# A gate's last 32 inner columns: small tiles against four copies in two f32r terms

## The reference, cut to what matters

```python
h = jnp.tanh(xx @ A).reshape(5, B * T, 32)
miu = jnp.einsum('smk,skc->smc', h, Bp).reshape(5, B, T, C) + lam
x5 = x[None] + b_a[None] * miu
...
g = jnp.tanh(g_in @ Wg1) @ Wg2
y = wkv6(r, k, v, w, u)
...
return yn * g @ Wo.T
```

## Time and profile before

| | us |
|---|---|
| median of 3 runs | 668.16 |
| the three runs | 666.41, 668.16, 670.31 |
| the profiled execution, its own time | 671.27 |
| its span, first to last instruction | 670.0 |
| TensorE matmul busy | 575.6 (86%) |
| TensorE weight load busy | 490.5 (73%) |
| VectorE busy | 433.1 (65%) |
| ScalarE busy | 280.8 (42%) |
| GpSimd busy | 221.2 (33%) |
| mean granted clock of TensorE | 0.929 of full speed |

### The profile page before, as it was taken

How to read it: one execution, slowest core, us unless ns; L and a number is a source line. 1 busy time by engine, 2 the same in 40 slices (tenths; PEclk the granted TensorE clock), 3 DMA queues, 4 the chain that set the end, 5 groups by cost and what they waited for, 6 DMA issues and landing times.

```text
span 670.0 us, 19207 instructions
## 1 busy us (share of the span) xinstructions
PE 575.6 (86%) x7602; PEld 490.5 (73%) x7602; DVE 433.1 (65%) x1091; ACT 280.8 (42%) x596; POOL 221.2 (33%) x178
## 2 busy tenths in 40 slices
PE   2799471649689999999999989999989999989795
PEld 1688351528478979898989878989878989777674
DVE  5784571626576767676767686767686767686432
ACT  3576020021235454545454525454535454535331
POOL 3120037150413333333333323433333333332413
PEclk9889575677699999999999999999999999999989
DMA  8988893280212323333333323333223333121422
GB/s 275 248 257 225 238 302 122 74 233 15 54 25 65 64 65 60 70 57 72 58 71 57 72 41 65 65 65 64 65 42 65 65 66 65 26 41 26 64 32 32
DMA packets 61962, 61.42 MB, mean 92 GB/s; under 512 B 6321, under 2 KB 56242, under 8 KB 61730
## 3 DMA queue, kind: packets, MB, share of 16 engines
q1 hardware_dynamic: 48002, 45.31, 25.5%
q0 software_dynamic: 12896, 14.50, 14.7%
q10 hardware_dynamic: 976, 0.38, 0.2%
HBM read 41.36 MB, written 23.14 MB: 96 GB/s over the span
## 4 chain that ended last, share of the span: by engine, by line
PE 70%; DVE 10%; issue 6%; SPq 5%; DMA 3%; another core or an unknown queue 3%; POOL 2%; ACT 1%; DVEq 0%; ACTq 0%; POOLq 0%
PE F L563 11%; PE F L555 10%; PE G L376 7%; PE LL L444 6%; PE YB L532 4%; PE YB L488 4%; PE G L345 4%; PE G L392 3%; PE YB L486 3%; PE G L407 2%; SPq L1539 2%; PE YB L513 2%; PE YB L517 2%; DVE mix L865 2%
## 5 line engine op out<-in xcount | busy, mean ns | idle before, releaser
L1417 POOL DMA_INDIRECT out<-ys,dst_row x39 | 65.7, 1685 | 208.9 <-DVE ys L981 196.0
L901 DVE COPY_PREDICATED AP_<-msk,LL 128x256 f32<-128x256 uint32 x96 | 51.2, 533 | 59.4 <-PE LL L444 37.2
L865 DVE SCALAR_TENSOR_TENSOR mix<-G,vec,ba 128x256 f32<-128x256 f32 x160 | 69.6, 477 | 25.8 <-PE G L345 15.4
L555 PEld LDWEIGHTS F<-xsT,w1s 128*128 128x128 f32 x624 | 73.8, 192 | 7.4 <-issue 5.4
L563 PE MATMUL F<-w,hsT 128*128 x312 | 78.1, 394 | 0.8 <-ACT hsT L1268 0.8
L555 PE MATMUL F<-xsT,w1s 128*128 128x128 f32 x624 | 78.2, 278 | 0.7 <-ACT xsT L1250 0.7
L1268 ACT ACTIVATE hsT<-F,b1c 128x128 f32<-128x128 f32 x156 | 44.7, 368 | 67.8 <-PE F L555 67.7
L444 PEld LDWEIGHTS LL<-R,K 64*64 64x64 f32 x2560 | 47.9, 139 | 31.1 <-issue 20.0
L444 PE MATMUL LL<-R,K 64*64 64x32 f32 x2560 | 56.6, 226 | 15.9 <-DVE D L919 12.3
L563 PEld LDWEIGHTS F<-w,hsT 128*128 128x128 f32 x312 | 58.2, 193 | 10.1 <-issue 1.4
L917 DVE TENSOR_TENSOR R<-R,D 128x256 f32<-128x256 f32 x112 | 48.4, 432 | 25.0 <-issue 19.9
(11 more groups left out here) (149 smaller groups left out, 1098.4 us busy)
## 6 DMA issues: line engine op xcount, KB each, us to landing
cd<-cd_d SPq DMA_DIRECT2D x32, 320.0 KB
w<-in_W SPq DMA_DIRECT2D x16, 512.0 KB, 8.9
cd_d<-cd SPq DMA_DIRECT2D x32, 160.0 KB, 3.3
b2t<-in_b SPq DMA_DIRECT2D x39, 128.0 KB
w<-in_x SPq DMA_DIRECT2D x8, 512.0 KB, 9.8
xn_d<-w SPq DMA_DIRECT2D x8, 512.0 KB
out<-in_x SPq DMA_DIRECT2D x8, 512.0 KB
out<-res POOLq DMA_DIRECT2D x16, 256.0 KB, 4.5
```

The source lines that it names most:

```text
L555: i1 = pe.matmul(FB[:, k * P:(k + 1) * P], w1s[:, cc, k, :], xsT[:, cc, :], start=(cc == 0), stop=(cc == 1))
L865: i1 = dve.scalar_tensor_tensor(mixed_in(u, c, n, cc), bk[:, cc * UN:(cc + 1) * UN], cvec(LAM + CC * n, cc), ba[:, cc, :, :].rearrange("p ...
L901: dve.copy_predicated(to, m, now.rearrange("p g (n t) -> p g n t", t=B)).then_inc(s["a"])
L1417: pool.indirect_dma_start(io["out"], bass.IndirectOffsetOnAxis(dst_row[:, f:f + 1], 0), ys[:, f % 2, :], None, compute_op=ALU.add).then_in ...
```

## The change

The last 32 inner columns are laid out four times on the host: `Wg1` becomes 256x256 (its last 32 columns four times) and `Wg2` 256x256 (its last 32 rows four times). `gate_down` is then four f32 products of 128x256, the second two of which give four copies of the rest's 32 rows on 128 partitions, for all tokens. The tanh covers 512 columns. ScalarE copies the rest's half of it, rounded to f32r, into `tgh`, which lies where `con` held its triangle and ones. VectorE's `gate_terms` makes `tgx` from it: in copies 1 and 3 the difference to the rounded value, in copies 0 and 2 the value itself, rounded (the factor is a new column LOW of `con`, 0 or -1). `Wg2`'s copies are brought to two terms as well: raw rows go to the still unused `sq`, VectorE casts them to f32r into `wg2x` and puts the difference to the rounded value in rows 64 to 127, once, in `centred`. The product of `tgx` and `wg2x` over 128 rows is then the sum of the four term pairs, as two f32r products of 128x256 in `gate_up`, in place of eight small f32 ones. `gate_up` waits for `gate_terms` (semaphore tx) where it waited for the tanh, and the copy waits for the terms of the unit before (tx) since `tgh` is single. SP issues three loads fewer.

```diff
-        wg1 = sb("wg1", [P, CC, GR])
-        wg2 = sb("wg2", [P, 2, C])
+        wg1 = sb("wg1", [P, CC, 2 * P])
+        wg2x = sb("wg2x", [P, C], F32R)
+        wg2 = sb("wg2", [P, C])
...
-        tg = sb("tg", [P, 2, UN + UB * QT])
+        tg = sb("tg", [P, 2, 2 * UN])
+        tgx = sb("tgx", [P, 2, UN], F32R)
...
+        tgh = con[:, TRI:TRI + UN]
...
             def gate_down(u, c):
...
-                for cc in range(CC):
-                    pe.matmul(bk[:, 0:UN], wg1[:, cc, 0:P], mixed_in(u, c, 4, cc), start=(cc == 0), stop=(cc == 1))
-
-                for cc in range(CC):
-                    for g in range(4):
-                        i1 = pe.matmul(bk[LORA * g:LORA * (g + 1), UN:UN + UB * QT], wg1[:, cc, P:GR], mixture(u, c, 4)[:, cc, :, QT * g:QT * (g + 1)],
-                                       start=(cc == 0), stop=(cc == 1), tile_position=(0, LORA * g))
+                for k in range(2):
+                    for cc in range(CC):
+                        i1 = pe.matmul(bk[:, k * UN:(k + 1) * UN], wg1[:, cc, k * P:(k + 1) * P], mixed_in(u, c, 4, cc), start=(cc == 0), stop=(cc == 1))
...
             def gate_up(u, c):
                 q = seq(u, c)
-                pe.wait_ge(s["tg"], q + 1)
+                pe.wait_ge(s["tx"], q + 1)
+                if not q:
+                    pe.wait_ge(s["gx"], 2)
...
-                    for g in range(4):
-                        at = slice(QT * g, QT * (g + 1))
-                        i1 = pe.matmul(BB[at, b * C:(b + 1) * C], tg[at, u, UN + QT * b:UN + QT * (b + 1)], wg2[at, 1, :],
-                                       start=False, stop=(b == UB - 1), tile_position=(QT * g, QT * g))
+                    i1 = pe.matmul(BB[:, b * C:(b + 1) * C], tgx[:, u, b * P:(b + 1) * P], wg2x[:, :], start=False, stop=(b == UB - 1))
...
             def centred():
...
+                raw = sq[:, 0, :]
+                dve.tensor_copy(wg2x[:, :], raw).then_inc(s["gx"])
+                dve.wait_ge(s["gx"], 1)
+                at = slice(2 * LORA, 4 * LORA)
+                dve.tensor_tensor(wg2x[at, :], raw[at, :], wg2x[at, :].bitcast(F32), ALU.subtract).then_inc(s["gx"])
...
+            def gate_terms(u, c):
+
+                dve.wait_ge(s["th"], seq(u, c) + 1)
+                rest = tg[:, u, UN:2 * UN]
+                dve.scalar_tensor_tensor(tgx[:, u, :], tgh, con[:, LOW:LOW + 1], rest, ALU.mult, ALU.add).then_inc(s["tx"])
...
                 mixed(u, c + 1, 0)
                 added(u, c + 1, 0)
+                gate_terms(*v)
                 mixed(u, c + 1, 1)
...
                 if q > 1:
                     act.wait_ge(s["gg"], q - 1)
-                act.activation(tg[:, u, :], bank(u, c, "tg")[:, 0:UN + UB * QT], ACT.Tanh).then_inc(s["tg"])
+                act.activation(tg[:, u, :], bank(u, c, "tg")[:, :], ACT.Tanh).then_inc(s["tg"])
+                act.wait_ge(s["tg"], q + 1)
+                if q:
+                    act.wait_ge(s["tx"], q)
+                act.activation(tgh.bitcast(F32R), tg[:, u, UN:2 * UN], ACT.Copy).then_inc(s["th"])
...
-                    (wg2[:, 0, :], io["Wg2"][0:P, :]), *((wg2[LORA * g:LORA * (g + 1), 1, :], io["Wg2"][P:GR, :]) for g in range(4)),
+                    (wg2[:, :], io["Wg2"][0:P, :]), (sq[:, 0, :], io["Wg2"][P:2 * P, :]),
...
+    four = lambda w, axis: np.concatenate([w] + 3 * [np.take(w, range(P, GR), axis)], axis)
...
-        "Wg1": g["a_Wg1"], "Wg2": g["a_Wg2"], "Wr": g["f_Wr"], "br": g["f_br"].reshape(E),
+        "Wg1": four(g["a_Wg1"], 1), "Wg2": four(g["a_Wg2"], 0), "Wr": g["f_Wr"], "br": g["f_br"].reshape(E),
```

More of the change, by code:

```diff
@@ L34 @@
 UN = UB * P
-QT = P // 4
 NU = 2 * NCH
@@ L48 @@
 SPARE = 3 * P
-NCONST = SPARE + 1
+LOW = SPARE + 1
+NCONST = LOW + 1
 RANK8 = 0
@@ L179, in program @@
             "cr0 cr1 "
-            "ba mm m x tA tw tB d km k vm v rm r gm tg "
+            "ba mm m x tA tw tB d km k vm v rm r gm tg th tx gx "
             "ru lev a gr big spread "
@@ L512, in gate_up @@
                 for b in range(UB):
-                    pe.matmul(BB[:, b * C:(b + 1) * C], tg[:, u, b * P:(b + 1) * P], wg2[:, 0, :], start=(b == 0), stop=False)
+                    pe.matmul(BB[:, b * C:(b + 1) * C], tg[:, u, b * P:(b + 1) * P], wg2[:, :], start=(b == 0), stop=False)
                 for b in range(UB):
-                    for g in range(4):
-                        at = slice(QT * g, QT * (g + 1))
-                        i1 = pe.matmul(BB[at, b * C:(b + 1) * C], tg[at, u, UN + QT * b:UN + QT * (b + 1)], wg2[at, 1, :],
-                                       start=False, stop=(b == UB - 1), tile_position=(QT * g, QT * g))
+                    i1 = pe.matmul(BB[:, b * C:(b + 1) * C], tgx[:, u, b * P:(b + 1) * P], wg2x[:, :], start=False, stop=(b == UB - 1))
                 i1.then_inc(s["gg"])
@@ L622, in tensor_program @@
                     ln_logits(j - 1)
-            pe.wait_ge(s["w"], 256)
+            pe.wait_ge(s["w"], 208)
             mixed(0, 0, 0)
@@ L744, in centred @@
                 wv3 = wv[:, :, :].rearrange("p c (h i) -> p (c h) i", i=HEAD)
-                dve.wait_ge(s["w"], 256)
+                dve.wait_ge(s["w"], 208)
                 dve.tensor_reduce(mwv, wv3, AX.X, ALU.add).then_inc(s["step"])
@@ L1068, in vector_program @@
             levels(0, 0, 2)
+            gate_terms(0, 0)
             mixed(1, 0, 1)
@@ L1086, in vector_program @@
             c = NCH - 1
+            gate_terms(1, c)
             levels(1, c, 0, 1)
@@ L1329, in scalar_program @@
             exponentials()
-            act.wait_ge(s["w"], 256)
+            act.wait_ge(s["w"], 208)
             decay_down(0, 0)
@@ L1602, in constants @@
     con[:, SPARE] = 1 + TOK + a
+    con[:, LOW] = -(a // LORA % 2)
     msk = np.zeros((P, len(LEVELS), LEAF), np.uint32)
```

## The result

The changed kernel takes **659.73 us** (median of 4 runs, 657.43 to 665.0), the kernel before 668.32 (4 runs, three of them the ones on record above): ratio 0.9873, 95% interval 0.9824 to 0.9922. The forecast of 666.3 (662.8 to 670.6) was too high: right in sign, wrong in size. Two more jobs in which the kernel before takes 668 and 670 gave 0.9839 [0.9798, 0.9880] and 0.9846 [0.9807, 0.9885]. In two other jobs the kernel before takes 638.0, and the ratio is 0.9923 [0.9903, 0.9943] and 0.9930 [0.9905, 0.9954]. The expectations speak of two chips, which isn't shown: the later slower jobs ran on chips numbered 7, 1 and 1, the faster ones on 1 and 14, and the first job's has no number.

The account below looks back on a forecast made before the run. TensorE was taken to bound 13 of the 14 halves, with waits elsewhere. Halves -3.1, half 0 +0.7, start +0.3 and +0.2, end 0 gave -1.9 us: 668.16 to 666.3, range 662.8 to 670.6.

Parts of the forecast that it names:

- gate_down +0.50, gate_up -0.85: TensorE in each half: gate_down from 1.32 to 1.82 us, gate_up from 2.05 to 1.20, net -0.35 where TensorE is the bound.
- the factor of four: The skill's up to 4x for dimensions of 32 or less; by it the change would cost TensorE +0.12 us a unit.
- The small tiles also cost something around them: TensorE time of 0.05 to 0.1 us a unit that start-to-start times give to the small tiles' neighbours.
- the first rival: No waits for z and mix 1, small tiles cost extra, start hides its part: -5.4 us, 662.8; chance 0.25.
- z, +0.07 a half: TensorE's gated_back would wait about 0.07 us for VectorE's z in each half, as gate_up gets 0.85 shorter.
- ScalarE, nothing: Longer tanh and added copy, +0.62 us on ScalarE, cost nothing in three-tile halves: out still ends 0.16 ahead of key_back.
- Mix 1 in two-tile halves, +0.14: gate_terms delays VectorE's mixed 1 by 0.4 us in two-tile halves, making it 0.14 late for TensorE's product.
- Halves -0.28 and -0.14, together -3.1: Change per half in us: nine three-tile halves at -0.28, four two-tile ones at -0.14, all but half 0.
- All of it arrives: The first rival's title: waits do not appear and small tiles cost extra; -5.4 us, 662.8; chance 0.25.
- Half 0, +0.7: Half 0: shorter gate_up earns nothing behind a wait; longer gate_down, partly at the low clock, costs +0.7 us.
- Start, +0.3, +0.16, and "I take nothing" for the loaded stretches: Start: Wg2 operations less saved loads +0.3 us; tanh of unit (1,0) +0.16; gate_down during w1/w2 loading nothing, at most +2.
- The rival: Start, while w1 and w2 load: added VectorE and ScalarE operations cause one more wait of about 6.9 us, 673.2; chance 0.11.

Follow-up runs that it names:

- down_only: The kernel before with the new gate_down (four f32 products, tanh of 512 columns) and the old gate_up on 32x32 tiles: 669.68 us, ratio 1.0026.
- f32_both: The kernel before with the new gate_down, and gate_up as four f32 products with a quarter of the copied rows: 664.34 us, ratio 0.9946.
- after_pool: The changed kernel with gate_terms behind added 2, added 4 ahead of affine, GpSimd's subtraction and gather delayed and swapped: 655.61 us (slower job), 631.75 (faster).

## Why the prediction was wrong

- *gate_down +0.50, gate_up -0.85.* Right: +0.50 to 0.51 and -0.84. down_only and f32_both show each alone. The small tiles' measured worth decided, not the factor of four.
- *"The small tiles also cost something around them", put down as already in the start-to-start times.* Wrong: 0.11 a half lies behind them, in hidden, and went. It was part of the first rival, which had it right, at its size.
- *z, +0.07 a half.* The right wait, mis-sized: 0.18 in the slower jobs. gate_up and hidden moved the slot 0.95 forward, not 0.85. In the faster ones it is nothing, as z is 0.4 earlier there.
- *ScalarE, nothing.* Right: out ends at 343.75 and key_back starts at 343.93, 0.18 later, where 0.16 was forecast.
- *Mix 1 in two-tile halves, +0.14.* Right in size: those gained 0.13 less than the three-tile ones in the faster job. With gate_terms moved back (after_pool) they gained 0.05 of it.
- *Halves -0.28 and -0.14, together -3.1.* In the slower jobs the steady period fell by 0.30 and 0.16, which is the forecast, by two errors that cancel (-0.11 behind, +0.11 more wait): that is luck. One half was read for all, and the two long early periods of the kernel before, worth 1.1 us, were missed. (The steady period before was 33.58 from gate_up to gate_up; the window of 33.55 in the earlier trace rows was cut a little beside them.) In a faster job it fell by 0.46 and 0.33, which sums to the -5.4 of "All of it arrives", and 0.9923 is that rival's result.
- *Half 0, +0.7.* gate_down did come at the low clock in a faster job (3.38 us for 8 records, granted clock 0.54), but the three traces of the changed kernel in slower jobs have it at the high clock (1.89 for 8 records, 1.00); gated_back ahead of it waited 0.52 to 0.69 there, in place of 3.48. From gated_back to the next key_back the first of these took 6.11 us where the kernel before took 6.81: 0.7 less, not 0.7 more.
- *Start, +0.3, +0.16, and "I take nothing" for the loaded stretches.* The two operations on Wg2 took 0.29 and 0.42, near the 0.25 and 0.4 forecast, and up to 137 us the kernel was 0.14 late. The last is **the step that failed**. The stretch was priced at nothing with +2 as its upper end and no gain below, though no row named its cause; in the pair of profiles it gave back about 6 us, with the tanh of unit (1,0) 6.56 earlier. What made the signals late, and why they were less late with the new gate_down, stays open. The rival priced one such stand, and only as a loss. The range missed by 3.1 us, mostly for that reason.
- *End, 0.* It was -0.9 in the pair of slower profiles and 0 in the faster one; no run follows the 0.9 up.
- *What would make it wrong* named this: the first 184 us changed by more than 2 us.

## What to carry to other kernels

A stretch whose cause no row names can move either way when anything near it changes; it belongs in the range on both sides, with the length of one such stand. Start-to-start differences must be taken for the neighbours of a changed group too, not for the group alone. One period read in the middle doesn't stand for all: compare the starts of every half first. And ahead of any change of order on VectorE, look at what GpSimd runs at that moment: 0.1 us of shift (0.31 to 0.38 behind the gather's start) turned a 0.17 us operation into one of 1.75.

## What the hardware showed that was not expected

- The same kernel takes 668 or 638 us in different jobs, and nearly all of the 30 us lies between 98 and 151 us (read_out of unit (0,0) begins at 151.32 and 123.45). There ScalarE and VectorE wait for TensorE's results or for a releaser that the trace calls remote, and TensorE for nothing that the trace shows. Their DMA rates at its beginning are alike (349 and 349 GB/s from 98 to 104 us). The cause is open.
- Two f32r products of 128x256 hold TensorE for 0.42 to 0.43 us behind f32 ones, and two f32 ones ahead of them 0.78, where they hold it for 0.97 with f32 ones behind (f32_both); together 1.20, as the prediction summed them from the earlier trace rows.
- The order of whole-array products and column tiles within gate_down is worth 0.19 us a half (33.58 and 33.77).
